# A fused attention and Mamba kernel on one core: u times D is made in two halves of channels, and the order from x_proj to the first state is new

## The reference, cut to what matters

```python
xz = jnp.einsum('bsd,ed->bse', xn, in_proj_w)
x_in, z = jnp.split(xz, 2, axis=-1)
u = silu(conv(x_in) + conv_b)                       # 1024 rows x 1024 channels
x_dbl = jnp.einsum('bsd,ed->bse', u, x_proj_w)      # 96 columns
dt_r, B, C = jnp.split(x_dbl, [DT_RANK, DT_RANK + N], axis=-1)
dt = jax.nn.softplus(jnp.einsum('bsr,dr->bsd', dt_r, dt_proj_w) + dt_proj_b)
h = h * exp(dt_t * A) + (dt_t * u_t) * B_t          # step by step, 16 states a channel
y = sum over the states of h * C_t, + u * D_param
y = y * silu(z);  out = x + gate * (y @ out_proj_w.T)
```

## Time and profile before

| what | value |
|---|---|
| median of 3 runs | 6713.71 us (6713.31 to 6713.74) |
| time of the profiled execution | 6710.81 us |
| its span, first to last instruction | 6709.0 us |
| mean granted clock of TensorE | 0.947 |
| busy PE, DVE, ACT, POOL | 91%, 87%, 68%, 47% |

### The profile page before, as it was taken

The page is one execution under the profiler, slowest core; times in us unless marked ns, Lnnn a source line. Parts: engine busy times, 40 slices in busy tenths (PEclk is TensorE's granted clock), DMA queues, the critical chain, the costliest instruction groups (busy, mean ns, idle before and its releaser), DMA issues.

```text
span 6709.0 us, 114578 instructions
## 1 busy us (share of the span) xinstructions
PE 6107.8 (91%) x43104; PEld 3983.7 (59%) x43104; DVE 5862.3 (87%) x7115; ACT 4556.3 (68%) x6528; POOL 3156.5 (47%) x1538
## 2 busy tenths in 40 slices
PE   5998999988999889989899899998899988999876
PEld 2774558645585556845568455774558645685554
DVE  0788999799997999979999799988999799996995
ACT  2775678657785677846778467865778667785663
POOL 0104881068701786019840389205881068601883
PEclk8999999999999999999999999999999999999967
DMA  3525885368934689238873498535894368924775
GB/s 143 181 82 160 203 207 153 107 163 195 236 104 141 160 205 235 77 141 177 211 200 95 135 208 209 162 98 159 196 214 142 119 162 199 244 69 144 171 149 127
DMA packets 428533, 1087.52 MB, mean 162 GB/s; under 512 B 49560, under 2 KB 49688, under 8 KB 423792
## 3 DMA queue, kind: packets, MB, share of 16 engines
q1 hardware_dynamic: 249440, 656.81, 30.2%
q0 software_dynamic: 160144, 390.09, 29.8%
q10 hardware_dynamic: 18432, 33.56, 1.4%
HBM read 570.16 MB, written 241.71 MB: 121 GB/s over the span
## 4 chain that ended last, share of the span: by engine, by line
PE 66%; DVE 16%; issue 7%; DMA 5%; POOL 4%; ACT 2%; SPq 1%; DVEq 0%; POOLq 0%; ACTq 0%
PE ps L1240 38%; PE ps L1349 12%; DVE area_h L1161 9%; PE ps L1488 8%; PE ps L1290 3%; POOL area_s L690 3%; DVE area_acc L1171 3%; DMA area_acc<-area_w 2%; DMA z_keep<-z_st 1%; DMA k_stack<-qk_keep 1%; PE ps L1292 1%; DVE area_dt L1149 1%; DVE norm_st L998 1%; DVE area_h L1129 1%; PE ps L1435 1%
## 5 line engine op out<-in xcount | busy, mean ns | idle before, releaser
L690 POOL TENSOR_TENSOR area_s<-area_u,area_s 128x1024 f32<-128x1024 f32 x1024 | 2548.6, 2578 | 536.1 <-DVE area_u L1152 372.4
L1161 DVE TENSOR_TENSOR_SCAN area_h<-ps,area_s 128x1024 f32<-128x1024 f32 x1024 | 2341.1, 2286 | 48.0 <-POOL area_s L690 39.7
L1488 PEld LDWEIGHTS ps<-ident,area_h 128*128 128x128 f32 x8192 | 987.0, 150 | 796.5 <-DVE area_acc L1171 425.5
L1488 PE MATMUL ps<-ident,area_h 128*128 128x128 f32 x8192 | 1190.5, 292 | 231.1 <-DVE area_acc L1171 152.6
L812 ACT ACTIVATE area_s<-area_s,negmax 128x1024 f32<-128x1024 f32 x1024 | 1180.7, 1153 | 253.4 <-DVE negmax L1058 245.9
L1058 DVE CUSTOM_DVE_ANT_0 area_s<-ps,area_dt 128x1024 f32<-128x1024 f32 x1024 | 1243.6, 1216 | 102.7 <-PE ps L1240 102.0
L879 ACT ACTIVATE ps<-area_dt,negA 128x1024 f32<-128x1024 f32 x1024 | 1147.0, 1120 | 240.2 <-DVE area_h L1161 102.3
L678 POOL TENSOR_TENSOR area_s<-area_s 128x1024 f32<-128x1024 f32 x64 | 180.2, 2815 | 2306.9 <-ACT area_s L854 2306.9
L863 ACT ACTIVATE area_w<-ps,C_nat 128x512 f32<-128x512 f32 x1024 | 704.9, 688 | 703.2 <-PE ps L1488 668.2
L1349 PE MATMUL ps<-ident,area_s 128*128 128x128 f32 x8192 | 1066.9, 273 | 0.4
L1349 PEld LDWEIGHTS ps<-ident,area_s 128*128 128x128 f32 x8192 | 959.9, 141 | 140.6 <-issue 7.0
(11 more groups left out here) (124 smaller groups left out, 5413.4 us busy)
## 6 DMA issues: line engine op xcount, KB each, us to landing
area_acc<-area_w POOLq DMA_DIRECT2D x256, 1024.0 KB, 8.8
area_s<-b_rows SPq DMA_DIRECT2D x256, 512.0 KB, 5.3
q_stack<-qk_keep SPq DMA_DIRECT2D x512, 128.0 KB, 2.8
k_stack<-qk_keep SPq DMA_DIRECT2D x512, 128.0 KB, 3.1
area_s<-z_keep SPq DMA_DIRECT2D x72, 512.0 KB, 4.4
qk_keep<-q_stack SPq DMA_DIRECT2D x128, 256.0 KB, 4.8
qk_keep<-k_stack SPq DMA_DIRECT2D x128, 256.0 KB, 4.8
y_keep<-area_acc POOLq DMA_DIRECT2D x8, 4096.0 KB, 13.9
```

Source lines behind the costliest of these rows:

```text
L690: pool.tensor_tensor(dbu[:, dl % 2, :], U[:, k // (NS * DL) * DL + dl, :], bb[:, q, :], ALU.mult).then_inc(s_dbu.sem, 1)
L1161: v.tensor_tensor_scan(out=hs[:, q, dl, :], data0=banks(2 * (dl % 2)), data1=dbu[:, dl % 2, :], initial=0.0, op0=ALU.mult, op1=ALU.add).th ...
L1488: last = nc.tensor.transpose(ps[:, 4 + n % 2, dl * P:(dl + 1) * P], hs[:, r % 2, dl, n * P:(n + 1) * P], ident[:, :])
```

## The change

The product of u and D is made in halves of 512 channels. The transposes of a half are `u_tile(n, half)`, with banks 2 and 3 for channels 0 to 511 and banks 4 and 5 for the rest; `start_acc(n, half)` is the product with D. Half 0 is transposed between the products of x_proj, from the second one on. Half 1 is spread among the dt tiles and the first scans. `s_ut` and `s_ai` become one signal for each half. dt tiles 1, 2 and 3 get other banks (`DT_BANK`), and `project_dt(3)` now waits until dt tile 2 has been made, since both use banks 6 and 7. On ACT `soft(3)` and the third decay change places. SP's program has the same instructions; its store of `acc` waits for the eighth product of half 1.

```diff
-DT_BANK = (0, 2, 6, 4)
+DT_BANK = (0, 2, 6, 6, 0, 2, 6, 4)
...
-                        sp.wait_ge(*s_ai.at(b, NT))
+                        sp.wait_ge(*s_ai[1].at(b, NT))
...
                 decay_tile(0, 0, 1)
+                decay_tile(0, 0, 2)
                 soft(3)
-                decay_tile(0, 0, 2)
                 decay_tile(0, 0, 3)
...
+                def start_acc(n, half):
+
+                    dve.wait_ge(*s_ut[half].at(b, n + 1))
+                    v.tensor_tensor(acc[:, n, half * 512:(half + 1) * 512], ps[:, (2, 4)[half] + n % 2, :], D_bc[:, half * 512:(half + 1) * 512],
+                                    ALU.mult).then_inc(s_ai[half].sem, 1)
+
                 for n in range(NT):
-                    dve.wait_ge(*s_ut.at(b, n + 1))
-                    v.tensor_tensor(acc[:, n, :], banks(4 + 2 * (n % 2)), D_bc[:, :], ALU.mult).then_inc(s_ai.sem, 1)
-                    if n == 1:
-                        dve.wait_ge(*s_ct.at(b, 1))
-                        v.tensor_copy(C_nat[:, :, :], banks(2).rearrange("p (n c) -> p n c", n=NT)[:, :, DTR + NS:XD]
-                                      ).then_inc(s_cn.sem, 1)
-                        clip(0)
-                    if n == 3:
-                        clip(1)
-                dve.wait_ge(*s_ai.at(b, NT))
-                dve.wait_ge(*s_cn.at(b, 1))
+                    start_acc(n, 0)
...
+                clip(0)
+                dve.wait_ge(*s_ct.at(b, 1))
+                v.tensor_copy(C_nat[:, :, :], banks(2).rearrange("p (n c) -> p n c", n=NT)[:, :, DTR + NS:XD]
+                              ).then_inc(s_cn.sem, 1)
+                start_acc(0, 1)
+                clip(1)
                 dt_and_dtu(0)
                 clip(2)
                 dt_and_dtu(1)
-                clip(3)
+                start_acc(1, 1)
                 scan(0, 0, 0, 0)
                 dt_and_dtu(2)
+                clip(3)
                 scan(0, 0, 0, 1)
+                start_acc(2, 1)
+                start_acc(3, 1)
                 dt_and_dtu(3)
                 scan(0, 0, 0, 2)
+                for n in range(4, NT):
+                    start_acc(n, 1)
                 scan(0, 0, 0, 3)
...
+                def u_tile(n, half):
+
+                    if n >= 2:
+                        pe.wait_ge(*s_ai[half].at(b, n - 1))
+                    for k in range(DL):
+                        done = nc.tensor.transpose(ps[:, (2, 4)[half] + n % 2, k * P:(k + 1) * P],
+                                                   U[:, half * DL + k, n * P:(n + 1) * P], ident[:, :])
+                    done.then_inc(s_ut[half].sem, 1)
...
-                last.then_inc(s_xd.sem, 1)
+                    if n == ND - 1:
+                        last.then_inc(s_xd.sem, 1)
+                    if n == 1:
+                        pe.wait_ge(*s_c0.at(b, 6))
+                        pe.wait_ge(*s_u.at(b, DL))
+                    if n:
+                        u_tile(n - 1, 0)
+                u_tile(NT - 1, 0)
...
+                pe.wait_ge(*s_xde.at(b, 1))
+                project_dt(0)
+                pe.wait_ge(*s_ai[0].at(b, NT))
+                for m in range(NT):
...
+                last.then_inc(s_ct.sem, 1)
+                pe.wait_ge(*s_c0.at(b, ND))
+                u_tile(0, 1)
+                u_tile(1, 1)
+                pe.wait_ge(*s_cn.at(b, 1))
+                project_dt(1)
+                project_dt(2)
+                u_tile(2, 1)
+                u_tile(3, 1)
+                pe.wait_ge(*s_dt.at(b, 3))
+                project_dt(3)
+                for n in range(4, NT):
+                    u_tile(n, 1)
+                pe.wait_ge(*s_ai[1].at(b, NT))
...
-                project_dt(2)
-                project_dt(3)
```

More of the change, by code:

```diff
@@ L396, in build @@
         s_cn = sig("c_ready", 1)
-        s_ut = sig("u_transposed", NT)
-        s_ai = sig("acc_started", NT)
+        s_ut = [sig(f"u_transposed{h}", NT) for h in range(DG)]
+        s_ai = [sig(f"acc_started{h}", NT) for h in range(DG)]
         s_dp = sig("dt_projected", ND)
@@ L1128, in clip @@
                     dve.wait_ge(*s_dp.at(b, n + 1))
-                    v.tensor_scalar(dtmp[:, n % DL, :], banks(DT_BANK[n % DL]), col("dtb", n), 30.0,
+                    v.tensor_scalar(dtmp[:, n % DL, :], banks(DT_BANK[n]), col("dtb", n), 30.0,
                                     ALU.add, ALU.min).then_inc(s_dm.sem, 1)
@@ L1134, in _ @@
                 dve.wait_ge(*s_x1s.at(b, 16))
+                def start_acc(n, half):
+                    dve.wait_ge(*s_ut[half].at(b, n + 1))
+                    v.tensor_tensor(acc[:, n, half * 512:(half + 1) * 512], ps[:, (2, 4)[half] + n % 2, :], D_bc[:, half * 512:(half + 1) * 512],
+                                    ALU.mult).then_inc(s_ai[half].sem, 1)
                 for n in range(NT):
-                    dve.wait_ge(*s_ut.at(b, n + 1))
-                    v.tensor_tensor(acc[:, n, :], banks(4 + 2 * (n % 2)), D_bc[:, :], ALU.mult).then_inc(s_ai.sem, 1)
-                    if n == 1:
-                        dve.wait_ge(*s_ct.at(b, 1))
-                        v.tensor_copy(C_nat[:, :, :], banks(2).rearrange("p (n c) -> p n c", n=NT)[:, :, DTR + NS:XD]
-                                      ).then_inc(s_cn.sem, 1)
-                        clip(0)
-                    if n == 3:
-                        clip(1)
-                dve.wait_ge(*s_ai.at(b, NT))
-                dve.wait_ge(*s_cn.at(b, 1))
+                    start_acc(n, 0)
                 def dt_and_dtu(n):
                     dve.wait_ge(*s_dl.at(b, n + 1))
-                    v.scalar_tensor_tensor(out=dT[:, n % DL, :], in0=banks(DT_BANK[n % DL]), scalar=col("dtb", n),
+                    v.scalar_tensor_tensor(out=dT[:, n % DL, :], in0=banks(DT_BANK[n]), scalar=col("dtb", n),
                                            in1=dtmp[:, n % DL, :], op0=ALU.add, op1=ALU.max).then_inc(s_dt.sem, 1)
@@ L1176, in _ @@
                 dt_and_dtu(1)
-                clip(3)
+                start_acc(1, 1)
                 scan(0, 0, 0, 0)
                 dt_and_dtu(2)
+                clip(3)
                 scan(0, 0, 0, 1)
+                start_acc(2, 1)
+                start_acc(3, 1)
                 dt_and_dtu(3)
                 scan(0, 0, 0, 2)
+                for n in range(4, NT):
+                    start_acc(n, 1)
                 scan(0, 0, 0, 3)
+                for half in range(DG):
+                    dve.wait_ge(*s_ai[half].at(b, NT))
+                dve.wait_ge(*s_cn.at(b, 1))
                 with dve.Fori(0, NS // 2 - 1) as i:
@@ L1403, in project_dt @@
                     for th in range(TB):
-                        done = mm(ps[:, DT_BANK[n % DL] + th, :], wdt[0:DTR, n * P:(n + 1) * P],
+                        done = mm(ps[:, DT_BANK[n] + th, :], wdt[0:DTR, n * P:(n + 1) * P],
                                   xdT[0:DTR, th * 512:(th + 1) * 512], 0, 0)
                     done.then_inc(s_dp.sem, 1)
[L1408 to L1424, removed]
@@ L1425, in _ @@
-                pe.wait_ge(*s_ai.at(b, NT))
+                pe.wait_ge(*s_xde.at(b, 1))
+                project_dt(0)
+                pe.wait_ge(*s_ai[0].at(b, NT))
+                for m in range(NT):
+                    last = nc.tensor.transpose(ps[:, 2 + m // 4, (m % 4) * P:(m % 4 + 1) * P],
+                                               xdT[:, m * P:(m + 1) * P], ident[:, :])
+                last.then_inc(s_ct.sem, 1)
+                pe.wait_ge(*s_c0.at(b, ND))
+                u_tile(0, 1)
```

## The result

The changed kernel takes 6799.2 us in the median of four runs (6793.4 to 6809.2), against 6713.5 for the kernel before; the ratio is 1.013 with a 95% interval of 1.0113 to 1.0148. By this ratio it is slower by about 87 us, and the forecast was 95 us with a range of 68 to 121. The profiled execution took 6804.4 us with a span of 6802.6, 93.6 us more than the span of before.

The account below looks back on a forecast made before the run. PE and DVE were taken to carry 82% of the chain, with a hidden store-and-load chain becoming exposed. Eight sequences at +11.9 us gave +95 on 6713.7, so 6809 us, range 6782 to 6835.

Parts of the forecast that it names:

- dt product 3, at the low clock: TensorE, four product instructions started only after dt tile 2, at 1.2 GHz: 3.62 us against 1.91.
- wait of VectorE ahead of clip 3: VectorE's gap while dt product 3 runs on TensorE: 2.5 us.
- transposes of h start: TensorE, behind the flips that wait for the loads: 634.9 instead of 621.80, +13.1 us a sequence.
- given back by the clock: TensorE's clock rises 5.2 us after the restart, so part of the products behind runs faster: 13.1 becomes 11.9 us.
- second sum: VectorE's sum that waited for TensorE at 627.89 comes at 639.8: +11.9 us a sequence.
- The mechanism: SP's store of acc, issued 22.6 us later, delays the loads, then the flips and transposes of h on TensorE.
- Its slack: Store and loads could come nearly 9 us later before delaying the transposes of h; 4.7 us against the flips.
- The early first state: VectorE's first scan begins at 603.0 instead of 607.59, 4.6 us won, then given back by later steps.
- The mis-sized term: Clock level after TensorE's restart: about half the saving on four product instructions, 3.62 us low and 1.88 full.
- The hidden store: Rival: transfers stay hidden, only the new order counts, scan 4 ends 3.3 us later; 6721 to 6740, 5%.
- The lasting gain of the first state: Rival: the 4.6 us won at the first scan last to the transposes of h; 6677, 3%.
- the longer stall: Rival: more piles up behind the transfers, on ACT and the transfer engines; 15 to 18 us a sequence, around 6845, 6%.

Follow-up runs that it names:

- run 1: Kernel before, with SP's store of acc issued only after the third scan of group 0, nothing else moved: 6778.1 us, ratio 1.0092.
- run 2: Kernel before, with SP's store of acc issued only after the first scan: 6706.6 us, ratio 0.9991.
- Run 4: Changed kernel with half 0 kept among the x_proj products, half 1 in one piece before dt tile 0, the rest about as before: 6721.8 us, ratio 1.0011.
- run 3: Changed kernel with half 1 made for even time tiles first and the store split, loads following the even tiles' store: 6733.6 us, ratio 1.0029.
- run 5: The kernel of run 3 with VectorE's third and fourth product of half 1 moved ahead of clip 3: 6720.4 us, ratio 1.0013.
- run 8: Changed kernel with one edit undone, soft(3) again ahead of the third decay on ACT: 6803.9 us, ratio 1.0141.
- run 6: Kernel before, dt product 0 moved ahead of the x_proj result's transposes and clip 0 ahead of the copy of C: 6700.7 us, ratio 0.9982.
- run 7: Run 6 with the later store of run 2, issued after the first scan: 6696.6 us, ratio 0.9977 against the kernel before.

## Why the prediction was right

Step by step, forecast against the trace of after (its times less 1.54):

| step | forecast | measured |
|---|---|---|
| copy of `xdT` starts | 588.55 | 588.51 |
| first scan starts | 603.0 | 603.33 |
| dt product 3, at the low clock | 3.62 us | 3.78 us |
| wait of VectorE ahead of clip 3 | 2.5 us | 2.61 us |
| store issued | 622.9 | 623.3 |
| loads issued | 630.3 | 630.5 |
| flips start | 633.0 | 633.4 |
| transposes of h start | 634.9 (+13.1) | 635.1 (+13.3) |
| given back by the clock | 1.2 us | 1.6 us |
| second sum | +11.9 | +11.75 |

*The mechanism* was right, and run 1 shows it by itself: a chain of two transfers that no wait of the kernel before named. *Its slack*, "nearly 9 us" against the transposes of h, was 9.7 us by runs 1 and 2. That the flips alone had only 4.7 us of slack never mattered, since they stood idle ahead of the fourth scan anyway.

*The early first state*, a gain of 4.6 us in the forecast, was there (4.3) and was worth nothing, as forecast. VectorE has the same work up to the fourth scan in either order, and putting the products with D behind the first scan only moves them. Run 4 shows that half 0 among the x_proj products doesn't pay either, even with the exchange at clip 0 kept.

*The mis-sized term* is small and lies in the clock. The forecast let half of the four product instructions run at the low level; they took 2.12 us in all, close to the full level's 1.88. The granted clock by stretch in the kernel after (columns as in the earlier trace rows):

```profile
606.00:612.00 6.00, 3.75 (x5) 1.16 (x4) 3.54 (x3) 1.12 (x1) 3.13 (x2) 0.50 0.00 0
...
624.00:630.00 6.00, 0.10 (x1) 0.00 (x0) 5.07 (x3) 0.00 (x0) 2.88 (x3) 0.50 0.66 247
...
636.00:640.00 4.00, 4.00 (x17) 3.19 (x16) 2.05 (x2) 3.60 (x5) 0.00 (x0) 0.64 0.59 195
640.00:644.00 4.00, 4.00 (x23) 2.69 (x22) 3.74 (x3) 2.02 (x4) 2.36 (x1) 1.00 0.01 3
```

0.64 over 636 to 640 is the lower level for 2.9 us and the full one for 1.1. The rise therefore came near 638.9, about 3.9 us after the restart at 634.93, where the forecast had 5.2. Over the eight sequences it came 4.5 to 5.3 us after the restart in the kernel before and 2.7 to 3.9 in the changed one. So the term of what the clock gives back was 1.2 us and measured 1.6. It made up for transposes of h that came 0.2 us later than forecast; that the sum is off by only 0.15 us is partly luck.

The prediction weighed a rule of the Trainium skill (page "TensorE: Matmul & The Clock Gate", section "HAM oscillation — how this bites in real kernels"), that a TensorE waiting for transfers between short pieces of work comes back at half its clock and pays on each return. The trace agrees that it comes back so: the granted clock is 0.50 from 630 to 636, and the flips take 1.94 us. It does not bear out the 1.2 us that were put on it. TensorE was at the low level at this place in the kernel before too, and the stretch at that level after the restart became shorter, not longer. dt product 3 was at the low level as well (3.78 us), but behind a wait for VectorE.

The other sizes: 87 us by the runs and 94 by the profiled executions, against 95. The forecast time, 6809, is 10 us over the median of 6799 and near the profiled 6804. The rivals are settled. The hidden store is out by run 1. The lasting gain of the first state is out by the result itself, and the longer stall by 11.75 us a sequence.

What stays of the loss without the stall is 21 us (run 3). Run 4 gives 7 to 9 of it to half 0 among x_proj (with the exchange at clip 0), run 5 some 9 to the wait for dt product 3 at the low clock. The last products' two-bank waits (0.61 and 0.16 us ahead of the last two products in runs 3, 5 and 8) are of the right size for the rest, but were not tried apart.

## What to carry to other kernels

Before an instruction is moved behind others, follow each of its signals to the queues as well as to the engines. Here the product with D was free to come later for VectorE, but SP's store waited for the last of the eight, and store, load and flip behind it had 9.7 us of slack that no wait in the trace showed. Where the bound is one engine's total work up to a point, an earlier first result is worth nothing; only its gaps are, and filling two of them by exchanging two places (run 6) did more than the whole new order.

## What the runs showed of the hardware

The granted clock did not depend on the length of the last pause alone. In the first sequence of run 6 the last two dt products, issued after a pause of 1.32 us, took 6.43 us:

```profile
598.96 6.43 PE L1240 MATMUL ps<-xdT,wdt 64*128 64x512 f32 x8 [1.32 <-DVE area_acc L1137]
```

In the other seven sequences of run 6, and in all eight of run 7 with the same order of the engines, they took 3.70 us after the same pause. The kernel before has both within one execution: 3.70 us in two sequences, the first among them, and 4.6 to 5.1 in the other six. The row of its second sequence, and under it the stretch around it, columns as in the earlier trace rows:

```profile
1402.65 4.59 PE L1240 MATMUL ps<-xdT,wdt 64*128 64x512 f32 x8 [1.32 <-DVE area_acc L1137]
...
1402.00:1408.00 6.00, 4.59 (x8) 1.56 (x8) 5.89 (x6) 2.68 (x3) 2.36 (x1) 0.78 0.70 264
```

In these six the clock fell while the products ran, though TensorE had had no pause over 1.32 us since the x_proj products began. In the first sequence, from which the forecast read its clock, it fell in the idle stretch behind them. The rise differs as well: in run 6 it came 2.7 to 6.0 us after the transposes of h restarted, behind the same 4.10 us of idle time. So what hangs on this clock differs between executions and between the sequences of one execution, here by 2.7 us for one group of eight instructions, and one sequence is not enough to read it from.
